# Order of single and double rounds within a head turned round

## The reference

```python
xn = _layernorm(x)
q, k, v = split(xn @ Wq + bq), split(xn @ Wk + bk), split(xn @ Wv + bv)   # 4 x 16 heads x 2048 x 16
q, k = _rope(q), _rope(k)
weights = softmax(q @ k.T / sqrt(256))            # 2048 x 2048 for each of 64 heads
attn = concat(weights @ v) @ Wo + bo
h = relu(s0 * [xn, -xn] @ sign(k0)) * 2           # 256 -> 1024
h = relu(s1 * h @ sign(k1)) * 2                   # 1024 -> 1024
ffn = s2 * h @ sign(k2)                           # 1024 -> 256
out = x + attn + ffn
```

## Time and profile before

| | us |
|---|---|
| median of 3 runs | 2860.54 (2855.91 to 2862.17) |
| the profiled execution | 2858.66 |
| its span, first to last instruction | 2856.9 |
| PE busy | 2667.9 (93%) |
| ACT busy | 2116.3 (74%) |
| DVE busy | 1076.9 (38%) |
| mean granted TensorE clock | 0.970 |

### The profile page before, as it was taken

The page is one execution under the profiler, slowest core; times in us unless marked ns, Lnnn a source line. Parts: engine busy times, 40 slices in busy tenths (PEclk is TensorE's granted clock), DMA queues, the critical chain, the costliest instruction groups (busy, mean ns, idle before and its releaser), DMA issues.

```text
span 2856.9 us, 55682 instructions
## 1 busy us (share of the span) xinstructions
PE 2667.9 (93%) x20423; PEld 1311.5 (46%) x20423; DVE 1076.9 (38%) x1689; ACT 2116.3 (74%) x2301; POOL 373.0 (13%) x309
## 2 busy tenths in 40 slices
PE   6777299999999999999999999999999999999997
PEld 3443144444444444444444444444444444444544
DVE  7999532323232323333233323232332323332323
ACT  4445288787878877787878787877778787878783
POOL 5788400000000000000000000000000000000000
PEclk9889699999999999999999999999999999999998
DMA  6666521212111212222222212121222222221213
GB/s 198 192 197 194 149 53 50 57 49 54 45 47 47 73 48 63 54 56 60 54 71 57 71 45 71 44 79 48 63 53 55 60 54 72 57 72 47 76 36 100
DMA packets 279715, 212.13 MB, mean 74 GB/s; under 512 B 183616, under 2 KB 227392, under 8 KB 272960
## 3 DMA queue, kind: packets, MB, share of 16 engines
q1 hardware_dynamic: 271040, 200.30, 25.7%
q10 hardware_dynamic: 8448, 8.39, 0.9%
HBM read 132.08 MB, written 76.55 MB: 73 GB/s over the span
## 4 chain that ended last, share of the span: by engine, by line
PE 83%; issue 2%; DVE 1%; DMA 1%; SPq 0%; POOL 0%; ACT 0%; DVEq 0%; POOLq 0%
PE ps_o L920 34%; PE ps_f L955 25%; PE ps_s L905 22%; PE ps_f L968 2%; DVE heads L1044 1%; PE ps_f L1013 0%; DMA q_rows<-row_shift 0%; DMA probs<-rest_sum_d 0%; DVE k_rows L1129 0%; PE ps_o L1013 0%; POOL heads L1032 0%; PE ps_f L996 0%; DMA heads_t<-heads 0%; SPq L694 0%; ACT probs L881 0%
## 5 line engine op out<-in xcount | busy, mean ns | idle before, releaser
L881 ACT ACTIVATE probs<-ps_s 128x1024 f32<-128x1024 f32 x2048 | 1956.4, 1026 | 524.0 <-PE ps_s L905 516.7
L920 PE MATMUL ps_o<-probs,v_ones 128*32 128x512 f32 x8192 | 1035.5, 604 | 10.0 <-issue 3.7
L905 PE MATMUL ps_s<-q_rows,k_rows 50*128 50x512 f32 x4096 | 838.6, 439 | 60.0 <-DMA q_rows<-row_shift 32.6
L905 PEld LDWEIGHTS ps_s<-q_rows,k_rows 50*128 50x128 f32 x4096 | 361.2, 185 | 750.7 <-ACT probs L881 628.0
L1087 DVE TENSOR_SCALAR h_hi<-ps_f 128x512 fp32r<-128x512 f32 x224 | 153.6, 686 | 826.3 <-PE ps_f L955 826.3
L955 PE MATMUL ps_f<-h_hi,ffn_w 64*128 64x512 f32 x2048 | 411.0, 397 | 0.0
L955 PE MATMUL ps_f<-h_lo,ffn_w 64*128 64x512 f32 x2048 | 405.6, 391 | 0.0
L920 PEld LDWEIGHTS ps_o<-probs,v_ones 128*32 128x32 f32 x8192 | 194.8, 108 | 434.0 <-issue 366.7
L1032 POOL TENSOR_TENSOR heads<-heads,sums 128x512 f32<-128x512 f32 x64 | 82.0, 1282 | 2128.3 <-DVE sums L1053 2128.3
L1044 DVE COPY heads<-ps_o 128x512 f32<-128x512 f32 x64 | 44.3, 692 | 553.8 <-PE ps_o L920 553.8
L1053 DVE RECIPROCAL sums<-sums 128x128 f32<-128x128 f32 x256 | 224.7, 919 | 0.6
(11 more groups left out here) (95 smaller groups left out, 1429.6 us busy)
## 6 DMA issues: line engine op xcount, KB each, us to landing
k_rows<-k_parts SPq DMA_DIRECT2D x128, 256.0 KB
q_rows<-q_parts SPq DMA_DIRECT2D x384, 64.0 KB
q_parts<-parts SPq DMA_DIRECT2D x32, 512.0 KB, 3.7
k_parts<-parts SPq DMA_DIRECT2D x32, 512.0 KB, 4.6
k_rows<-k_parts SPq DMA_DIRECT2D x128, 128.0 KB
x_chunk<-in_x ACTq DMA_DIRECT2D x16, 512.0 KB, 4.2
xn_t<-xnT SPq DMA_DIRECT2D x16, 512.0 KB, 4.4
v_heads<-v_sb SPq DMA_DIRECT2D x16, 512.0 KB, 5.4
```

The lines of the kernel that those rows point to most:

```text
L881: nc.scalar.activation(probs[:, s % PBUF, half * 2 * C:(half + 1) * 2 * C], ps_s[:, half].rearrange("p c n -> p (c n)"), ACT.Exp, scale=SC ...
L905: last = nc.tensor.matmul(ps_s[:, half, w], k_rows[rows, u, t * P:(t + 1) * P], q_rows[rows, u, half], start=True, stop=True)
L920: last = nc.tensor.matmul(ps_o[32 * c:32 * c + 2 * DH], v_ones[:, u, t], probs[:, s % PBUF, c * C:(c + 1) * C], start=(t == 0), stop=(t == ...
```

## The change

`ROUNDS` is made from another list of bursts. Before, a head was single, double, five times, then the closing single: steps 0 / 1-2 / 3 / 4-5 / ... / 12 / 13-14 / 15. After, it is double, single, five times, then the closing single: steps 0-1 / 2 / 3-4 / 5 / ... / 12-13 / 14 / 15. The visits stay in the doubles and in the closing single, in the same order and number, and so does the rule for what a round contains. Around the end of a head the order was double (13-14), closing single (15), single (0), double (1-2); it becomes double (12-13), single (14), closing single (15), double (0-1). `PROJECT_AT` goes from 8 to 7, so `project` stays in a single, now that of step 11 in place of step 12. The number of rounds is unchanged.

```diff
-PROJECT_AT = 2 * 4
-ROUNDS = [(KT * j + t, n) for j in range(HEADS) for t, n in
-          [(3 * k + m, m + 1) for k in range(KT // 3) for m in range(2)] + [(KT - 1, 1)]]
+PROJECT_AT = 2 * 4 - 1
+BURSTS = (2, 1) * (KT // 3) + (1,)
+ROUNDS = [(KT * j + sum(BURSTS[:n]), BURSTS[n]) for j in range(HEADS) for n in range(len(BURSTS))]
```

## The result

| | median us | runs | ratio to before (95% interval) |
|---|---|---|---|
| kernel before | 2859.39 | 5 | |
| changed kernel | 2911.58 | 5 | 1.0183 (1.0171 to 1.0194) |

The changed kernel is 52 us slower. Its profiled execution has a span of 2909.8 us against 2856.9, a granted clock of 0.966 against 0.970.

What follows compares the result with a forecast made beforehand. PE was taken as the bound by a small margin, held up by ACT when score halves stand close. 48 x 0.52 = 25.0, plus 13.4, plus 4.8, gave +43.2 us: 2903, range 2871 to 2920.

Steps and rivals of the forecast that it cites:

- The copy wait removed: Ends of heads inside a pass: a double's scores and visits cover DVE's copy of ps_o, gaining 0.18 us at each of 48.
- The wait for ACT: Closing single: its second score half waits for ACT's second exponential, losing 0.70 us each time, bounded by 0.30 and 0.81.
- The turns: From pass to pass: 13 turns with a gap lose 1.03 us each (13.4), two without lose 2.40 each (4.8).
- the forecast wait of 0.33: At the 13 turns with a gap: the first visit waits for DVE's last two sums, losing 0.33 us each.
- the high end of the range: Whole kernel: 2919, with the stall at 0.81 (7 more) and half a dozen more low-clock turns (9 more).
- The clock rival: Closing single: its new idle lowers the clock each time, 48 x 1.5 = 72 us on top, 2976; chance 0.05.
- The two rivals of a refund: Later doubles within a head repay the 0.70: faster with the full copy gain, 2847 (chance 0.08), or about 2860 (0.07).
- That the copy would not be covered: Ends of heads: the change does not remove the copy wait, 8.6 us more, 2912; counted inside the main case.

Runs made afterwards that it cites:

- visit between the halves: Changed kernel with the visit of the closing single moved between its two score halves (visit = m in place of m - 1): 2859.42 us, ratio 1.0006 to the kernel before.
- second copy: Changed kernel with ps_o copied twice at the end of a head, first to sums, which is overwritten right after: 2918.36 us, ratio 1.0213 to the kernel before.
- best kernel of all: Changed kernel with single first in each pass's last head, closing single's visit between its score halves, and a pass's last two sums before the copy: 2846.69 us, ratio 0.9964.
- old order in head 3: Changed kernel with the old order of rounds (single first) in the last head of each pass, PROJECT_AT 7: 2899.34 us, ratio 1.0146 to the kernel before.
- old order in head 0 and the visit between: Changed kernel with single first in each pass's first head, PROJECT_AT 8, and the closing single's visit between its score halves: 2862.38 us, ratio 1.0019.

## Why the prediction was right, step by step

The forecast was +43.2 us of span, 2903, range 2871 to 2920; measured +52.9, 2911.6. The main mechanism held. The 9.7 us that were missing are +10.1 at the turns, -2.6 inside passes and +2.2 ahead of the first copy and behind the last.

*The copy wait removed.* 0.18 us each was forecast. The visit between the halves isolates it: 0.18, 0.20 and 0.20, 9 us against 8.6. That it is covered is shown by the second copy that costs nothing inside passes.

*The wait for ACT.* 0.70 us each was forecast; 3.03 - 2.36 = 0.67 in the timeline, 0.62 to 0.70 when the visit is moved. In part this is luck, since two small errors cancel. I had the second half start 0.18 after ACT's end and 1.04 after the first half; it starts 0.05 after it (1102.18 against 1102.13) and 0.92 after the first, so only 0.92 - 0.34 = 0.58 is lost up to there. The other 0.1 comes behind it. The first visit follows the start of the closing single by 1.26 (1102.52) where it followed by 0.57 in the kernel before (1085.81), 0.69 more. The rows of the two first visits, the kernel before and then the changed one:
```profile
1085.81 0.40 PE L955 MATMUL ps_f<-h_lo,ffn_w 64*128 64x512 f32 x2
```
```profile
1102.52 0.40 PE L955 MATMUL ps_f<-h_lo,ffn_w 64*128 64x512 f32 x2
```

The three rounds take 9.61, forecast 9.65. No refund came: the double behind takes 4.89 (1104.29 to 1109.18), exactly as before. The reason that I gave, that ACT is idle before each single, shows in the row of 1100.19 (0.98). Inside passes the sum is 22.4 against 25.0, because the last distance of the last pass has no such wait and became shorter, and because the others grew by 0.47 to 0.52.

*The turns.* Here the sum was too small. Beside the 15 x 0.70 I had put 7.7; it was 28.3 - 10.5 = 17.8. At the two turns without a gap the wait was as worked out (first visit 2.63 us after the scores, forecast 2.65), but the clock fell after it: 3.78 each against 2.40. At the 13 others the forecast wait of 0.33 did not come at all, because the gap, which I left as it was, grew by 5.9 / 13 = 0.45. These 13 grew by 20.7 us: 8.7 are the wait for ACT, 5.9 the gaps, and the other 6 agree with the price of the clock that the ten turns from pass 4 on show. More turns at the lower clock I had only in the high end of the range. So the total is partly luck too: a wait of 13 x 0.33 = 4.3 us that was put in and did not come stands against 5.9 us of longer gaps that were left out.

*The clock rival* was wrong in its place and right in kind: inside passes the idle of 0.4 us at each closing single never lowered it, while at the turns it fell more often than before. *The two rivals of a refund* fall with the unchanged double. *That the copy would not be covered* falls with the second copy.

## What to carry to other kernels

Where two engines hand a small buffer back and forth, look at what stands between two fillings of the same half, and not only at the wait that the list names: moving work to cover a wait of 0.2 us laid bare one of 0.7 that the same work had been covering. The cheapest cure was not another order of rounds but one visit of independent work put between the two halves; the best kernel of all, 2846.69 us, has a mixed order as well. Where a loop's end and beginning change with an order, count the turns apart: besides the wait that is the same at every end of a head, a third of the loss (17.8 of 52.9 us) was there, and no row of a steady period shows it.

## What the runs showed of the hardware

The gap on PE at a taken branch of these loops is not a constant. Its mean in one execution is 1.9 to 2.5 us (24.3 to 33.1 over 13), and the single gaps of all kernels run from 1.5 to 3.7 us. It tends to be longer with single, closing single ahead of the branch; why stays open.

The granted clock does not follow from the length of one idle. At the two turns without a branch, PE stood still for 2.05 to 2.73 us before the first visit in four kernels: the changed one, the visit between the halves, the changed one with the second copy, and the old order in head 3. In six of these eight cases the lower level followed (0.50, 1.2 GHz); in two it did not. In the other eight kernels that idle is not there, and the clock stayed up at all 16 such turns. One of the two cases, with the visit between the halves, at the turn from pass 14 to 15:
```profile
2671.06 0.51 PE L955 MATMUL ps_f<-xT_hi,ffn_w 64*128 64x512 f32 x2 [2.05 <-DVE rest_sum L1066]
```
```profile
2672.00:2674.00 2.00, 2.00 (x18) 1.23 (x14) 2.00 (x3) 1.07 (x2) 0.00 (x0) 1.00 0.16 41
2674.00:2676.00 2.00, 2.00 (x20) 0.51 (x18) 1.97 (x4) 1.90 (x2) 1.29 (x1) 1.00 0.14 57
```

It is the same at the branches: a gap of 1.82 us in the kernel before was followed by the lower level, and one of 3.12 us in the kernel with the old order in head 0 and the visit between was not. What the lower level costs is steadier: about 1.5 us for a stretch of 3.4 us in the kernel before.
